# Two-way scan layer: broadcast row of B in front of the sums, preparation between their halves, y read a pair later, one group of silus a forward stage

## The reference

```python
        def _mamba(xf, Win, conv_w, conv_b, Wx, Wdt, bdt, A_log, D, Wout):
            ...
            xz = jnp.einsum('blc,ec->ble', xf, Win)
            u, z = jnp.split(xz, 2, axis=-1)
            ...
            u = jax.nn.silu(jnp.swapaxes(conv, 1, 2) + conv_b)
            x_dbl = jnp.einsum('bld,ed->ble', u, Wx)
            ...
            delta = jax.nn.softplus(jnp.einsum('blr,dr->bld', dt, Wdt) + bdt)
            dA = jnp.exp(jnp.einsum('bld,dn->bldn', delta, A))
            dBu = jnp.einsum('bld,bln,bld->bldn', delta, Bm, u)
            def step(h, inp):
                dA_l, dBu_l, C_l = inp
                h = dA_l * h + dBu_l
                y = jnp.einsum('bdn,bn->bd', h, C_l)
                return (h, y)
            ...
            y = y + u * D
            y = y * jax.nn.silu(z)
            return jnp.einsum('bld,od->blo', y, Wout)
```

## Time and profile before

| | |
|---|---|
| median of 3 runs | 10609.8 us (10602.0 to 10616.06) |
| profiled execution | 10616.89 us |
| its span | 10615.1 us |
| mean granted TensorE clock | 0.968 |
| the two-way scan's pairs, first to last scan | 7012.7 to 10526.2 us |
| busy over the span: PE / DVE / ACT / POOL | 9717.4 / 8515.8 / 8057.9 / 5905.9 us |

### The profile page before, as it was taken

How to read it: one execution, slowest core, us unless ns; L and a number is a source line. 1 busy time by engine, 2 the same in 40 slices (tenths; PEclk the granted TensorE clock), 3 DMA queues, 4 the chain that set the end, 5 groups by cost and what they waited for, 6 DMA issues and landing times. The chain is left out here.

```text
span 10615.1 us, 137498 instructions
## 1 busy us (share of the span) xinstructions
PE 9717.4 (92%) x45956; PEld 5177.6 (49%) x45956; DVE 8515.8 (80%) x8102; ACT 8057.9 (76%) x14637; POOL 5905.9 (56%) x2628
## 2 busy tenths in 40 slices
PE   9999999999899999999999999988888888888885
PEld 6767767677444444444444444433333333333332
DVE  7858858578599999999999411159999999999997
ACT  5646646466488888888888555579999998888885
POOL 0000000000288888888888300058989988889885
PEclk9999999999899999999999999989999999999997
DMA  1000000000145555545555100035555555555556
GB/s 41 0 1 0 0 0 0 0 0 0 61 173 175 175 175 174 177 174 174 176 174 177 66 8 8 8 120 184 186 184 179 187 182 189 184 186 188 183 187 220
DMA packets 335957, 1241.58 MB, mean 117 GB/s; under 512 B 38672, under 2 KB 38800, under 8 KB 331792
## 3 DMA queue, kind: packets, MB, share of 16 engines
q1 hardware_dynamic: 335472, 1235.51, 34.7%
HBM read 1145.18 MB, written 56.62 MB: 113 GB/s over the span
## 5 line engine op out<-in xcount | busy, mean ns | idle before, releaser
L951 POOL TENSOR_TENSOR l_hc<-l_h,l_hc 128x1024 f32<-128x1024 f32 x1024 | 2398.8, 2365 | 451.5 <-DVE l_h L1049 451.0
L1841 POOL TENSOR_TENSOR l_ring<-l_ring 128x1024 f32<-128x1024 f32 x1024 | 2429.7, 2397 | 347.4 <-DVE l_ring L1919 341.3
L1919 DVE TENSOR_TENSOR_SCAN l_ring<-l_ring,l_carry,l_ps 128x1024 f32<-128x1024 f32 x960 | 2200.1, 2333 | 1.3
L688 PE MATMUL l_ps<-l_hc,w_sb 128*128 128x512 f32 x4096 | 1936.4, 595 | 69.1 <-POOL l_hc L951 61.7
L1049 DVE TENSOR_TENSOR_SCAN l_h<-l_decay,l_carry,l_ps 128x1024 f32<-128x1024 f32 x768 | 1760.3, 2334 | 4.3 <-issue 0.4
L1545 PE MATMUL l_ps<-l_ring,w_sb 64*64 64x512 f32 x8192 | 1216.9, 667 | 343.0 <-POOL l_ring L1841 334.4
L116 POOL COPY l_qm<-l_q 128x128 f32 x128 | 82.7, 648 | 2576.4 <-PE l_ps L188 2179.5
L829 ACT ACTIVATE l_decay<-l_delta,w_sb 128x1024 f32<-128x1024 f32 x1024 | 1152.8, 1138 | 168.8 <-DVE l_h L1049 168.6
L1731 ACT ACTIVATE l_xt<-l_duT,l_BT 128x128 f32<-128x128 f32 x4096 | 1246.0, 388 | 0.0
L842 ACT ACTIVATE l_xt<-l_duT,l_BT 128x128 f32<-128x128 f32 x4096 | 1245.9, 388 | 0.0
L212 PE MATMUL l_ps<-l_attnT,l_vT 128*128 128x128 f32 x8192 | 1095.7, 277 | 1.3 <-ACT l_attnT L283 1.3
(11 more groups left out here) (233 smaller groups left out, 15001.6 us busy)
## 6 DMA issues: line engine op xcount, KB each, us to landing
l_hc<-l_rows_dram SPq DMA_DIRECT2D x1024, 512.0 KB, 3.7
l_ring<-l_rows_dram SPq DMA_DIRECT2D x1024, 512.0 KB, 4.8
l_crossed<-l_delta SPq DMA_DIRECT2D x128, 256.0 KB, 5.3
l_gate_dram<-l_gate SPq DMA_DIRECT2D x32, 512.0 KB, 7.1
l_recon_dram<-l_recon SPq DMA_DIRECT2D x32, 512.0 KB, 5.4
l_gate<-l_gate_dram SPq DMA_DIRECT2D x32, 512.0 KB, 6.0
l_xw<-x_dram SPq DMA_DIRECT2D x30, 513.5 KB, 7.3
x_dram<-x SPq DMA_DIRECT2D x16, 512.0 KB, 2.6
```

What stands on the lines that cost most here:

```text
L688: ins = nc.tensor.matmul(y_sum[:, half(j)], ident, hc[:, unit % CS, half(j)], start=q == 0, stop=q == S1 - 1)
L951: nc.gpsimd.tensor_tensor(hc[:, unit % CS, :], h[:, unit % HS, :], hc[:, unit % CS, :], ALU.mult).then_inc(hc_done, 1)
L1841: nc.gpsimd.tensor_tensor(hc[:, unit % CS, :], h[:, unit % HS, :], hc[:, unit % CS, :], ALU.mult).then_inc(hc_done, 1)
L1919: nc.vector.tensor_tensor_scan(h[:, unit % HS, order], decay[:, unit % DS, order], x_now[:, order], before, ALU.mult, ALU.add).then_inc(sc ...
```

## The change

Five places in the loop move, and nothing is computed otherwise:

- On TensorE, a pair's order was `turn_back(P)`, the pieces, first half sum of P - 1, `broadcast_B(P + 1)`, second half sum. It becomes `turn_back(P)`, `broadcast_B(P + 1)`, first half sum, the pieces, second half sum.
- On VectorE, `add_y` stood after both scans of r 0; it stands between the even and the odd scan of r 1.
- On GpSimd, `gating` goes from r 1 to r 2.
- On ScalarE, in forward stages, the group of silus in r 2 becomes two plain copies (`raw_u` with the bias, `raw_z`) without table loads; `silu_raw` applies the silu to them in SBUF, in place, in the group of r 4.
- TensorE's waits in r 3 and 4 go by the copies (`gate_raw`, `u_raw`) instead of the silus, since it is the copies that free the banks.

```diff
@@ tensor @@
                     if r in (3, 4) and n < 4 * NK:
                         if r == 3 and forward(K):
-                            pe.wait_ge(gate_out, 2 * S + 1)
+                            pe.wait_ge(gate_raw, S + 1)
...
                     if r == 4 and forward(K):
-                        pe.wait_ge(u_out, n + 1)
+                        pe.wait_ge(u_raw, S + 1)
                         project_z(S, 1)
...
                 for P in range(NS * PAIRS):
                     turn_back(P)
-                    pieces(*divmod(P, PAIRS))
+                    if P + 1 < NS * PAIRS:
+                        broadcast_B(P + 1)
                     if P:
                         add_pair(P - 1, 0)
-                    if P + 1 < NS * PAIRS:
-                        broadcast_B(P + 1)
+                    pieces(*divmod(P, PAIRS))
                     if P:
                         add_pair(P - 1, 1)
@@ scalar @@
+                def raw_u(n):
+                    K, e, j = n // 4, n // 2 % 2, n % 2
+                    act.wait_ge(u_mm, n + 1)
+                    at_least(act, y_out, 2 * K + e - 3)
+                    nc.scalar.activation(u[:, K % 2, e, half(j)], [U, V][j], ACT.Identity, bias=col("conv_b", e)).then_inc(u_raw, 1)
+
+                def raw_z(S, j):
+                    act.wait_ge(z_mm, 2 * S + j + 1)
+                    at_least(act, gated_ready, S - 1)
+                    at_least(act, gate_stored, 16 * (S - 1))
+                    nc.scalar.activation(gate[:, S % TI, half(j)], [V, U][j], ACT.Identity).then_inc(gate_raw, 1)
+
+                def silu_raw(S, n):
+                    K, e, j = n // 4, n // 2 % 2, n % 2
+                    own = u[:, K % 2, e, half(j)]
+                    act.wait_ge(u_raw, S + 1)
+                    nc.scalar.activation(own, own, ACT.Silu).then_inc(u_out, 1)
+                    own = gate[:, S % TI, half(0)]
+                    act.wait_ge(gate_raw, S + 1)
+                    nc.scalar.activation(own, own, ACT.Silu).then_inc(gate_out, 1)
...
                     if r == 2 and forward(K):
-                        silu_u(n)
-                        silu_z(S, 0)
-                        exp_set()
+                        raw_u(n)
+                        raw_z(S, 0)
                     if r == 4 and forward(K):
+                        silu_raw(S, n)
                         silu_u(n + 1)
                         silu_z(S, 1)
                         exp_set()
@@ gpsimd @@
-                    if r == 1 and S:
+                    if r == 2 and S:
                         gating(S - 1)
@@ vector @@
                     scan(P, 0)
+                    if r == 1 and S:
+                        add_y(S - 1)
                     scan(P, 1)
-                    if r == 0 and S:
-                        add_y(S - 1)
```

More of the change, by code:

```diff
@@ L1331, in two_way_scan_layer @@
         x_in = [sem(f"x_in_{i}") for i in range(3)]
-        u_mm = sem("u_mm"); u_out = sem("u_out"); z_mm = sem("z_mm"); gate_out = sem("gate_out")
+        u_mm = sem("u_mm"); u_raw = sem("u_raw"); gate_raw = sem("gate_raw"); u_out = sem("u_out"); z_mm = sem("z_mm"); gate_out = sem("gate_out")
         gate_stored = sem("gate_stored"); gate_loaded = sem("gate_loaded")
```

## The result

| | before | after |
|---|---|---|
| median | 10609.4 us (4 runs, 10602.0 to 10616.1) | 10741.8 us (4 runs, 10713.7 to 10752.4) |
| ratio to before, 95% interval | | 1.012 (1.0106 to 1.0134) |
| span of the profiled execution | 10615.1 us | 10742.4 us |
| mean granted TensorE clock | 0.968 | 0.958 |

The changed kernel is slower by 132 us, 1.2%. The forecast was 10622 us and its range ended at 10715: the time lies outside it, on the slow side.

What follows compares the result with a forecast made beforehand. VectorE was taken as busiest, with GpSimd's queue limiting odd stages. About 220 us of waits come back and nearly as much is spent again: +0.2 us a stage over 64 stages, +13 us on 10609.8, so 10622 us; range 10525 to 10715.

Steps and rivals of the forecast that it cites:

- the clock after `soft_max`: TensorE's slow start before pair 5's odd scan: 1.05 us odd stages, 0.9 even forward, 0.3 even backward; bounds 0 and 1.4.
- GpSimd's backlog: Even backward stages: both products of pair 3 still to come; odd scans of pairs 5 to 7 wait 1.8, 1.3, 0.4 us.
- The rows of C: Loads into slots freed later by the second half sum: 0.4 us in A of even stages, hidden where GpSimd is behind.
- A of stage 17: Odd forward stage, from the end of pair 1's even scan to the end of `soft_max`: 23.3 us.
- the queue of GpSimd: Products, gating, `split_rest` and `soft_low` on GpSimd set A in odd stages: sum 22.05 us before the change.
- The idle time before odd scans: Sign on VectorE: under 30 us in all would mean the forecast's TensorE chain is too long.
- B of stage 17: Odd forward stage, from the end of `soft_max` to the end of the next stage's pair 1 even scan: 33.0 us.
- The port against even stages: Slower rival: `soft_max` waits for both GpSimd products in even stages too, 2.4 us more each, 10697 us; chance 0.20.
- The port in odd stages: Faster rival: `soft_max` gets the port at the next gap in odd stages, 1.7 us in 32 stages, 10565 us; chance 0.10.
- ScalarE's pace: Faster rival: ScalarE sets the forward pace, so its 1.3 us saved show, 10580 us; chance 0.08.
- The clock holding: Faster rival: the low clock costs nothing in B, which loses 0.9 to 1.05 us in three of four kinds, 10560 us; chance 0.18.
- The smaller loss: Slower case: TensorE's or ScalarE's chains 0.5 to 1 us a stage longer than summed, 10650 to 10680 us; chance 0.17.

Runs made afterwards that it cites:

- 7x run: Changed kernel with `turn_back` of pair 4 repeated 7 times in odd stages, 4 in even forward, 3 in even backward: 10626.0 us, ratio 1.0015.
- changed: The kernel with all five moves of the change, against the kernel before: 10741.8 us, ratio 1.012.
- 5x and 3x run: Changed kernel with `turn_back` of pair 4 repeated 5 times in odd and 3 times in even stages: 10699.6 us, ratio 1.0073.
- run 13: Not a run's number: the text says that in the 5x and 3x run, 13 of these 16 even backward stages have no low level.
- sixth slot: Changed kernel with six slots instead of five for C's rows: 10685.9 us; with the pieces directly behind `turn_back` as well: 10537.3 us.
- three pairs of runs: Silus changed against not: kernel before 10607.2 against 10609.4 us, changed 10741.8 against 10730.8, pieces directly behind `turn_back` 10546.1 against 10539.6.

## Why the prediction was wrong, step by step

**The failing step is the term "the clock after `soft_max`".** The mechanism was named, with its place (the start after the pause, in the chain of pair 5); its size was not right. The step took 2.6 us at the low level, from how lay, and 40% of it, 1.05 us; over the layer the sum holds (0.9 + 1.05 + 0.1 + 1.05) x 16 = 50 us for it. Measured were 5.2, 5.5, 6.2 and 4.3 us at the low level in the four kinds of stage, and the 7x run, which ends most of the low level and leaves the chain as long as it was, gives back 116 of 132 us. So the term, with what follows from it, was short by some 66 of the 120 us by which the time exceeds the forecast.

Both of its factors were too small. The length came from a stretch that ended too early: the clock was still low at the end of the earlier trace rows, as the next stretch of the kernel before shows (length, PE's busy time, granted clock, then the DMAs' share and GB/s):

```profile
7983.00:7989.00 6.00, 6.00 (x34) 0.92 0.96 259
```

As the low level is half the clock, both stretches together have 2 x (0.21 + 0.08) x 6 = 3.5 us of it, which is where the upper bound of the term lay. The price was taken from a half sum of 1.70 us behind a broadcast that still ran at the full level (0.60 us); in changed one took 1.91 us to the next start, so that 47% of it are lost. 5.5 us x 0.47 = 2.6 us, and the odd forward stages have 3.47 - 0.79 = 2.7 us between changed and the 7x run.

It was not the longer pause as such. Two even forward stages of changed, 10 and 16, have the same pause and do the same work behind it without a gap:

```profile
7606.74 1.03 PE L1518 MATMUL l_ps<-l_stack,sel 96*128 96x512 bf16 x2 [3.31 <-DVE l_ring L1940]
7949.70 0.60 PE L1518 MATMUL l_ps<-l_stack,sel 96*128 96x512 bf16 x2 [3.31 <-DVE l_ring L1940]
...
7606.70:7613.00 6.30, 6.26 (x15) 2.03 (x16) 5.72 (x5) 2.55 (x4) 6.30 (x3) 0.53 0.02 7
7949.70:7956.00 6.30, 6.30 (x20) 2.00 (x24) 5.68 (x5) 3.35 (x6) 6.30 (x3) 0.73 0.01 5
```

The first ran 5.9 us at the low level and waited 3.58 us before pair 5's odd scan, the second 3.4 us and waited 2.44. Even backward stages paused for only 1.5 to 2.5 us and had the most of it, 6.2 us. The wait follows how much of the chain is slow; what sets that length these runs don't show.

**The places.** The waits before pair 5's odd scan exceed the predicted ones by 1.73, 1.62, 2.18 and 0.77 us, 6.30 x 16 = 101 us. In even backward stages 1.8 us of the forecast were GpSimd's backlog and only 0.1 the clock; in the 5x and 3x run 13 of these 16 stages have no low level there, and they wait 1.5 to 1.7 us, so the 1.8 were nearly right. The 1.3 and 0.4 us that I had before pairs 6 and 7 of these stages were 0 and 0.29, 23 us less over the layer. The 34 us before pair 0's odd scans, which went with the sixth slot, I had not at all.

**The rows of C** were the second mis-sized term. I had them at 0.4 us in even stages and hidden elsewhere. They are worth 56 us (six slots), and the reason is again the chain: the slot is freed by the second half sum, which I had at 4.8 us after the even scan and which in stage 17 ends 7.4 us after it (8015.0 from 8007.6), with `project_z` in front of it for 0.95. The 56 and the 116 overlap and must not be added: with the clock kept, 109 of the 279 us of waits for those loads are gone too.

**What held.** A of stage 17 was forecast at 23.3 and is 23.07; the queue of GpSimd in it was read rightly. Pair 3's wait for `project_z`, forecast at 0.8, is 0.79. The idle time before odd scans, of which I had written that under 30 us would mean too long a chain, is 283: the chain of the sum was too short. The waits before the even input went altogether. `soft_max` in odd stages was forecast at 6 to 7 us and takes 5.9 to 7.1, but for stage 21 with 1.6. The silus did nothing that could be told, as taken. B of stage 17 was forecast at 33.0 and is 34.15, with 2.81 instead of 1.85 before pair 5's odd scan and small leftovers. 16.2 of the 48.1 us before `add_y` stayed, which I had as gone but for 0.1.

**The rivals.** The port against even stages, my slow rival, did not occur: `soft_max` took 1.4 to 3.4 us there forward and 1.4 to 2.4 backward, far from the 5 that I had named for it. (Its sum had a slip: 22.5 and 33 make 55.5, not 55.7; the 10697 hardly moves by it.) The port in odd stages occurred in one of them, stage 21, and gained nothing there (5.3 us of wait before pair 5's odd scan). ScalarE's pace is refuted by three pairs of runs. The clock holding, which I gave 0.18 for a gain, is the one that turned out the other way round. The smaller loss that I had put beside the slow rival, chains of TensorE 0.5 to 1 us a stage longer and 10650 to 10680, is nearest to what happened, with 1.9 us a stage.

Why `soft_max` gets the port between two products in even stages and waits for both in nearly all odd ones is not settled. In stage 17 of changed:

```profile
7997.22 2.39 POOL L1836 TENSOR_TENSOR l_z<-l_z 128x1024 f32<-128x1024 f32 x1
7999.55 4.70 POOL L1862 TENSOR_TENSOR l_ring<-l_ring 128x1024 f32<-128x1024 f32 x2
```

`soft_max` started at 7999.35, in the last 0.26 us of `soft_low` (L1836), and ended at 8005.33, 1.1 us after the second product. The Trainium skill (SBUF — State Buffer, Who interferes with whom) has the later of two block until the earlier is finished. By that, `soft_max` would have run at 7999.6 and ended at some 8000.7, an estimate with the 1.1 us that it takes behind the products. Measured is a wait through `soft_low`'s end and two more products, so here the measurement decides: the rule gives the direction, not the length.

## What to carry to other kernels

Before you move an engine's work, count what stands between the event that wakes it and the instruction that others wait for, and take out of it what could be done before the event: the same moves of y and of the broadcast gave 10742 us with the preparation inside that chain and 10546 with it in front. A chain without slack turns every slow start and late slot into waiting, each of which looks like a cause by itself; with 2 us of slack neither the repeats nor a sixth slot gained anything that could be told. And don't price a slow start from one row: take the stretch until the clock is back at its full level, and look at the same place in many stages, where it lay between 3.4 and 6.8 us. Where moved work makes waits vanish and the time stays, look at the instructions that lengthened instead: `soft_max` took back 30 of 48 us in one run and grew by 71 us in another.

## What the runs showed of the hardware that I had not expected

After a pause of 6.42 us TensorE's next work ran at the low level for 4.4 us in stage 17 and, after 6.65 us, for some 6 us in stage 19, with half sums of 1.91 instead of 1.02 us and a convolution of 3.56 instead of 1.88; behind a pause of 1.47 us, with transposes up to it, the clock was at the full level. But the pause alone doesn't tell: equal pauses of 3.31 us were followed by 5.9 and by 3.4 us at the low level, and in 8 of 16 even backward stages of the 7x run a low stretch came up behind pauses of under 0.7 us. Useless transposes in the pause were worth 116 us, 1.1% of the kernel, though TensorE did more work. In the changed kernel they never paid for what better order gave: 10626 against 10546. Repeats and a sixth slot together in the changed order were not tried.
